# Constant products on TensorE between the last image's score steps, and new orders of the steps on all engines

## The reference

```
x = x + L0(gn(x))   # attention: 1024 queries x 256 keys (2x2 strided conv + layer norm), 8 heads of 32
x = x + L1(gn(x))   # layer norm, in_proj, 3x3 depthwise conv, selective scan (4 groups of 64 channels,
                    # state 1), layer norm, gate from a small MLP, projection
x = x + L2(gn(x))   # channel attention: softmax of 8 32x32 grams over the pixels, projection
x = x + L3(gn(x))   # s = relu(MLP(mean)); frac_b*maxpool[q+1] + frac_s*maxpool[q] + x,
                    # kernels 1,3,5,7,9,11,13, q = floor(s), for each image and channel
```

## Time and profile before

| | us |
|---|---|
| three runs | 741.39, 743.9, 744.7; median 743.9 |
| the profiled execution, its own time | 742.38 |
| span of its records | 740.5 |
| mean granted clock of TensorE in it | 0.917 of 2.4 GHz |
| busy: PE, DVE, ACT, POOL | 634.9, 545.4, 417.8, 35.5 |

### The profile page before, as it was taken

One profiled execution on the slowest core, in us unless ns is written; L12 is line 12 of the kernel. 1 busy time (PEld: TensorE's weight loads), 2 busy tenths in 40 slices (PEclk: granted clock), 3 DMA queues, 4 the chain that ended last, 5 costly groups with the idle time before them and its releaser, 6 DMA issues.

```text
span 740.5 us, 9520 instructions
## 1 busy us (share of the span) xinstructions
PE 634.9 (86%) x3472; PEld 303.2 (41%) x3472; DVE 545.4 (74%) x995; ACT 417.8 (56%) x703; POOL 35.5 (5%) x26
## 2 busy tenths in 40 slices
...
DVE  3477249523747466857789899987899998999696
...
GB/s 322 86 121 2 58 135 29 3 1 28 31 1 57 58 51 2 2 1 58 0 1 1 107 2 1 1 58 57 0 1 1 1 0 58 0 1 1 57 1 57
DMA packets 15855, 26.88 MB, mean 36 GB/s; under 512 B 3601, under 2 KB 7345, under 8 KB 15682
## 3 DMA queue, kind: packets, MB, share of 16 engines
...
...
## 4 chain that ended last, share of the span: by engine, by line
PE 62%; DVE 19%; ACT 12%; issue 4%; DMA 1%; ACTq 1%; SPq 0%; DVEq 0%
PE PSB L1665 14%; PE PSB L1795 9%; PE PSB L1776 6%; PE PSB L1686 4%; PE PSB L2075 4%; PE PSB L1699 3%; PE PSB L1809 3%; PE PSB L1741 3%; DVE NEGMAX L1185 3%; PE PSB L1761 3%; PE PSB L1909 2%; PE PSB L1876 2%; PE PSB L1841 2%; ACT PT L656 2%; ACT PS L753 2%
## 5 line engine op out<-in xcount | busy, mean ns | idle before, releaser
L1185 DVE TENSOR_REDUCE NEGMAX<-PSB 128x2 f32<-128x512 f32 x128 | 79.5, 681 | 22.8 <-PE PSB L1741 22.6
L656 ACT ACTIVATE PT<-PSB 128x512 f32<-128x512 f32 x128 | 67.4, 606 | 49.2 <-PE PSB L1761 49.0
L1795 PE MATMUL PSB<-XNP,WTAP 64*64 64x512 f32 x576 | 66.8, 616 | 2.6 <-issue 2.6
L1741 PE MATMUL PSB<-KST,QST 96*128 96x256 f16 x256 | 43.4, 320 | 10.8 <-DMA KST<-KL 7.7
L1761 PE MATMUL PSB<-QST,KST 98*128 98x512 f16 x128 | 38.8, 423 | 7.3 <-DMA QST<-ML 6.0
L1795 PEld LDWEIGHTS PSB<-XNP,WTAP 64*64 64x64 f32 x576 | 22.4, 139 | 45.3 <-issue 45.2
L1500 DVE TENSOR_TENSOR PA_<-HB 128x1024 f32<-128x1024 f32 x32 | 39.1, 1223 | 1.3 <-PE PSB L2075 0.6
L987 POOL TENSOR_TENSOR GA<-GA,PT 128x1024 f32<-128x1024 f32 x8 | 20.2, 2540 | 400.2 <-ACT PT L684 400.2
L1741 PEld LDWEIGHTS PSB<-KST,QST 96*128 96x128 f16 x256 | 25.7, 112 | 30.6 <-DMA KST<-KL 8.2
L720 ACT ACTIVATE U<-PSB 64x512 f32<-64x512 f32 x32 | 26.5, 829 | 20.5 <-PE PSB L1795 19.9
L1776 PE MATMUL PSB<-PT,VT 128*32 128x512 f32 x256 | 35.7, 630 | 1.8 <-issue 0.6
...
## 6 DMA issues: line engine op xcount, KB each, us to landing
...
```

The costliest lines, as they stand in the source:

```text
L656: e.activation(PROB[:, 4 * kt + j, :], bank("A", b, f"st{g}_{kt}_{j}")[:, :], ACT.Exp)\
L1185: e.tensor_reduce(NEGMAX[:, h, 2 * j:2 * j + 2], bank("A", b, f"s{h}_{j}")[:, :].rearrange("p (t k) -> p t k", t=2), AX.X, ALU.max, negate ...
L1741: mm = e.matmul(s[:, t * NK:(t + 1) * NK], QST[0:96, h, qt * P:(qt + 1) * P], KST[0:96, h, :], start=True, stop=True)
L1795: mm = e.matmul(banks[gi][64 * half:64 * half + 64, :], WTAP[rows, cc, tap(2 * cc + gi, dy, dx), :], XNP[rows, cc, dy + 16 * half:dy + 16 ...
```

## The change

The stream L on PE gets products with constant inputs. `keep_busy` multiplies the identity by two of the constant matrices (128 x 128 by 128 x 256, f32) into the bank that `acc0_0` overwrites later, so that their results are never read. For the last image alone 4 such products stand ahead of `gn3`, 3 ahead of `w1`, 1 ahead of `w2` and 3 ahead of `acc0_0`. The banks of acc0_0 are taken ahead of gn3 instead of ahead of acc0_0.

```diff
+            def keep_busy(b, n):
+
+                e.wait_ge(mats_loaded, 16)
+                for _ in range(n):
+                    e.matmul(bank("L", b, "acc0_0", 0)[:, 0:2 * P], mat("ident"), MAT[:, 1:3, :], start=True, stop=True)
+
             def stream_l(b):
-                yield from stream_m(b)
+                steps = stream_m(b)
+                if b == B - 1:
+                    for half in range(2):
+                        take("L", b, "acc0_0", act_l, f"o0_{half}", half)
+                for n in (4, 3, 1):
+                    if b == B - 1:
+                        keep_busy(b, n)
+                    next(steps)
+                    yield
+                if b == B - 1:
+                    keep_busy(b, 3)
                 for k in range(KPOOL):
                     for cc in range(CC):
-                        if k == 0:
+                        if k == 0 and not (b == B - 1 and cc == 0):
                             for half in range(2):
                                 take("L", b, f"acc0_{cc}", act_l, f"o{cc}_{half}", half)
...
 SP_ORDER = """
-F5 X1 A3 X1 F3 A3 X1 F3 A3 F3 A2 M1 A1 M5
+F3 X1 F2 A3 X1 F3 A3 F1 X1 F2 A3 F3 A2 M1 A1 M5
 """
 POOL_ORDER = """
-C6 W1 C2
+C8 W1
 """
```

More of the change, by code:

```diff
@@ L150 @@
 BANKS_N = """
-2
+0
 """
 BANKS_S = """
-2 4 2 - -
+2 0 1 - -
 """
 BANKS_F = """
-0 1 3 4 5 6 7 0 3 3 6 3 2 3 5 6 4 0 2 1 1 4 5 0 3 5 6 2 7 6 2 7 1 4 3 2
+0 1 3 4 5 6 7 0 1 7 4 5 1 2 6 3 5 1 6 6 4 7 2 5 3 5 3 6 1 7 5 6 7 0 3 6
 """
 BANKS_A = """
[L160 to L166, removed]
+3 4 2 5 6 7 0 1 3 4 2 5 6 7 3 4 2 0 1 5 6 7 3 4 2 0 1 5 6 7 3 4 2 01 5 6 3 4 - 7 5 6 2 3 1 0 7 6 2 3
+4 1 07 - 6 2 3 4 5 6 2 3 47 5 6 2 3 - 5 6 3 1 75 - 6 0 3 2 4 7 5 1 6 0 3 2 4 7 6 0 3 2 4 7 6 0 5 1 3
+2 4 7 6 2 0 4 5 71 6 2 3 0 - 1 6 7 3 1 4 7 3 1 5 4 7 0 72 - 3 1 5 0 1 5 0 2 31 7 5 0 2 - 7 5 6 0 27
+- 7 2 0 7 5 2 4 0 7 1 5 6 2 4 3 0 1 0 1 5 7 6 2 4 0 1 3 5 7 6 1 3 2 54 7 6 0 1 - 3 2 7 1 4 5 3 6 4 5
+3 0 6 54 - 0 6 0 0 2 0 0 1 07 4 1 3 6 - 1 2 6 7 45 - 1 4 3 6 1 4 5 3 7 6 1 4 2 5 0 3 6 3 6 1 7 4 2 5
+3 6 0 1 7 0 4 2 1 56 3 0 3 0 - 3 0 1 7 6 5 0 1 7 6 5 0 1 65 - 0 1 7 4 1 3 4 2 51 3 0 7 3 - 1 1 2 7
+32 -
 """
 BANKS_C = """
-1 7 3 2 1 3 0 0 4 6 3 0 2 6 0 3 7 2 7 1 5 6 7 2 4 0 3 3 1 0 7 6 2 7 3 2 1 3 0 4 0 4 3 5
+1 0 2 4 7 5 1 6 3 4 0 6 7 3 2 0 0 6 1 6 7 2 0 4 6 3 0 0 1 3 2 1 6 7 6 1 0 5 2 3 2 3 7 1
 """
 BANKS_B = """
[3 rows of a table removed]
[3 rows of a table added]
 """
 BANKS_D = """
-4 2 4 7 1 2 6 - 2 7 2 6 4 0 4 5 4 3 5 6 5 0 5 1 7 3 5 - 7 0 4 5 4 0 5 4 6 1 5 1 1 6 3 5 7 6 0 - 3 5
-6 0 4 3 7 1 5 3 6 4 2 7 1 3 5 7 1 - 3 5 7 1 3 5 7 1 3 6 2 0
+4 0 4 1 6 7 3 - 0 0 3 3 6 3 7 4 2 3 2 3 5 4 5 7 2 7 0 - 6 7 0 0 4 0 4 7 1 6 5 0 0 5 4 7 6 5 6 - 0 1
+5 6 4 3 0 5 1 0 3 2 5 4 6 1 0 4 6 - 1 0 4 6 1 0 4 6 1 3 5 0
 """
 BANKS_M = """
-2 0 7 6 7 2
+6 2 7 5 7 1
 """
 BANKS_L = """
-3 0 4 62 04 - - - - - - - - - - - - - - 4 5 7 13 62 - - - - - - - - - - - - - -
+3 7 2 35 72 - - - - - - - - - - - - - - 7 2 1 46 35 - - - - - - - - - - - - - -
 """
@@ L206 @@
-L1 D4 L4 D2 L15
+F14 A10 F1 A1 F1 A3 F3 A4 F1 A13 F1 A7 F1 A2 F3 C2 F2 C2 F1 C11 A7 C1 A3 C1 A1 B1 A2 C1 B1 C1 B1 A1
+F2 C6 B7 A3 B5 A1 B3 A1 F2 A6 B1 A8 B1 A7 B10 C1 F1 B2 C1 B2 C1 B1 C1 B1 C2 B4 C2 F1 C3 F1 B1 C2 B1
+C2 B1 F2 B1 C2 B3 D2 F1 C3 F1 D2 C5 D1 F2 D1 F1 D2 B3 D1 B1 D5 B10 A7 B1 A1 B1 A6 D1 A1 D2 B1 A3 B1
+D1 B1 A2 D1 A7 D2 A2 M1 A1 B1 F2 A8 M1 A2 B4 M2 B8 C1 B8 C1 F1 M1 F1 C2 F2 C2 F1 C1 B2 C6 B2 C2 B3
+C2 D1 F2 M1 D1 F1 C1 D2 F1 C7 F3 B2 D1 B1 D3 B1 D6 B10 A4 B1 A3 D1 A1 B3 A6 B2 A11 D2 A8 D1 A2 B2 D1
@@ L207 @@
+A1 B4 A2 B8 A1 B2 A1 B2 D1 B2 D1 B1 M1 B1 M1 B3 M1 B1 M1 B1 C2 D1 C2 D1 C2 D1 M1 D1 C11 D2 M1 D7 B3
+C3 B1 D1 B2 C5 B5 D1 B9 D1 B4 D1 B9 D1 B5 D1 B2 D2 B7 L2 D2 L2 D2 L4 D10 L1 D2 L1 D1 L1 D2 L2 D2 L17
 """
 DVE_ORDER = """
[L209 to L211 removed]
```

42 lines of the change are left out of this document (19 added, 23 removed), and 6 rows, old and new, of the table BANKS_B.

## The result

The changed kernel takes 731.8 us (four runs, 729.5 to 732.8) where the kernel before takes 744.3 in the same series: ratio 0.985, 95% interval 0.981 to 0.989. A second series gave 731.8 and 0.986 (0.983 to 0.988). So it is 11 us faster (the ratio's share of 744.3); I had forecast 739.9, some 3 to 4 faster, with a range down to 733.0. The direction was right, the size was not. One execution of norm2_only, a kernel further down, was in a slow state (1087 us) and is not counted.

What follows compares the result with a forecast made beforehand. Neither PE nor DVE was taken as a bound by itself; PE's waits, which step order can change, were the target. Terms −1.1 −2.9 −2.5 +1.5 +1.8 +0.6 −0.6 = −3.2 from 743.1 gave 739.9 us; range 733.0 to 747.0.

Steps and rivals of the forecast that it cites:

- The rest: Hundreds of other steps moving by one to ten places, all over the kernel: counted 0, ±2 us for their sum.
- Norm of image 2: Ahead of image 2's conv (378 to 395 us): ln_var1#2 passes L1124, PE's 2.56 us idle time goes; −2.5 us.
- Norm of image 0: 112 to 139 us: three statistics and L1056 leave DVE's queue ahead of ml0#1, so image 1's scores start earlier; −2.9 us.
- First maxima: Start, 38 to 54 us: eleven maxima ahead of DVE's setup and five behind, so mT0 comes earlier; −1.1 us.
- Last maxima: 453 to 466 us: L1265 and p2_1 move ahead of image 3's mx6 and mx7, so mT1#3 is late; +1.5 us.
- Norm of image 3: 537 to 547 us: acc1_0#1 stands ahead of n1 on DVE and may be held by POOL; +1.8 us.
- The memset: POOL's memset, moved from 476 us to behind c1_1#3, may hold acc1_0#1 and n1 on DVE; +0.6 us.
- The tail: Behind 699 us: constant products in PE's idle time raise the clock, ending L1500's wait for the weighted sum; −0.6 us.
- all gains stay: Rival: the gains all arrive and the losses lie beside the path; −7.1 us, 736.0 us, chance 0.20.
- Absorbed: Rival: PE's gains before 400 us are half lost where DVE is slower, losses stay; +0.1, 743 us, chance 0.20.

Runs made afterwards that it cites:

- norm2_only: Kernel before with one move: DVE's four statistics steps of image 3's conv go behind n1_1#2, the last norm step of image 2; 741.3 us, ratio 0.997.
- the cut at 401: Kernel before with the new orders for the first 401 us, the old orders behind, no constant products; 731.8 us, ratio 0.987.

## Why the prediction was wrong

The steps, by the table above.

- *The rest*, counted 0 with ±2, is the step that failed most: 154 to 377 gave −5.2 in the two profiled executions, and −4.4 as a mean of all traces (221.2 to 222.7 in five with the old order, 216.8 to 218.5 in ten with the new). It has no large place, only many of 0.4 to 1.4 (such as PE's waits of 1.43, 1.17, 0.38 and 0.84 from 271 to 276, which are 0.82, 1.22, 0.59 and 0.20 now). I had compared each moved step with the old end times and called it neutral where PE wasn't late; the sum of hundreds of such steps has a sign that this doesn't tell.
- *Norm of image 2*: "PE has just 2.56 to give" was wrong. The idle time went, and 1.7 of the conv at the lower clock with it. norm2_only gives 4.3 at this place. I had read the idle time in the earlier trace rows but not that its 32 records took 5.32.
- *Norm of image 0*: −4.1 for −2.9, again with 2.3 in PE's busy column. The clock there was 0.81 and is 0.92. I had not counted PE's gn0#2, which waits 2.00 ahead of the scores in the old order.
- *First maxima*: −1.1 forecast; two orders of the start can't be told apart. I had set "if the setup ends when it did", but the setup is a chain in which PE and DVE wait for each other by turns, and it now begins behind eleven maxima.
- *Last maxima*: +1.5 forecast, −0.9 for the stage, which is inside the spread of one order (2.6). mT1#3 came late as said (11.0 earlier than before, where its neighbours are 12 to 13 earlier), and the attention's last products fell back to −4. But PE made B's products in that time (−15 to −23), and by 490 both streams stood at −13. A late step costs only the time in which PE has nothing else.
- *Norm of image 3*: the step held, 1.5 for 1.8 at n1. The stage is even all the same, because PE's products in it took 1.2 less; what else gave the rest isn't separated.
- *The memset*: 0 for +0.6. *The tail*: −0.3 to −0.6 for −0.6, though the clock went from 0.50 to 0.87 in it.

The rival "all gains stay" had the right sign with 0.20 and still ended at 736. "Absorbed" fell with the cut at 401. The rivals' sums were made of the same terms as the forecast, so none had the clock behind the idle times, or the places that I had called neutral. The range was added up wrongly besides: all gains (−7.1), the rest at −2 and the first two terms at −2 and −4 give 732.0, not 733.0. That the sign came out right is partly luck: the two losses that I had counted for the last maxima and the memset aren't there, and some 40% of the gain is in what I had counted as nothing.

What stays open: how the gain between 154 and 377 is divided and which moves make it, and how much of the 11 us the clock holds. Between 108 and 413 PE is busy for 279.9 and 280.0 us in the two executions with the whole old order and for 273.6 to 276.4 in eight with the new, while the stretch is 304.8 and 304.9 against 291.0 to 292.8 long; so 3.5 to 6.4 of some 12 to 14 us are busy time.
